# Recommendation tower on one core: the last group of gathers split in two, and a layer-2 step moved between two quarters of products

## What is computed

```
combined = concat([dense[:, None, :], e], axis=1)            # 512 x 27 x 128
inter    = einsum('bnd,bmd->bnm', combined, combined)        # 512 x 27 x 27
z = concat([dense, inter[:, triu_i, triu_j]], axis=1)
h = relu(concat([z, dense], axis=1) @ W_top1 + b_top1)       # 607 -> 512
h = relu(h @ W_top2 + b_top2)                                # 512 -> 256
y = h @ W_top3                                               # 256 -> 1
```

## Time and profile before

| | |
|---|---|
| median of 3 runs | 103.61 us (103.44 to 103.71) |
| the profiled execution | 104.75 us, of which its span 102.9 us and 1.85 us around it |
| TensorE busy, matmuls / weight loads | 95.2 us (92%) / 78.5 us (76%) |
| VectorE, ScalarE, GpSimd busy | 53.9 us (52%), 49.5 us (48%), 62.1 us (60%) |
| chain that ended last | PE 59%, DVE 19%, issue 6%, DMA 5%, POOL 5%, ACT 2% |
| mean granted TensorE clock | 0.983 |

### The profile page before, as it was taken

How to read it: one execution, slowest core, us unless ns; L and a number is a source line. 1 busy time by engine, 2 the same in 40 slices (tenths; PEclk the granted TensorE clock), 3 DMA queues, 4 the chain that set the end, 5 groups by cost and what they waited for, 6 DMA issues and landing times.

```text
span 102.9 us, 3492 instructions
## 1 busy us (share of the span) xinstructions
PE 95.2 (92%) x1525; PEld 78.5 (76%) x1525; DVE 53.9 (52%) x123; ACT 49.5 (48%) x85; POOL 62.1 (60%) x66
## 2 busy tenths in 40 slices
PE   5999999998999999999996999999899899399990
PEld 2348674886888888899886888998789798297870
DVE  4599999999999998953001600280026110043200
ACT  2845899969847966794110342052205621004250
POOL 1588877777777777777777777777777720000000
PEclk9999999999999999999999999999999999966999
DMA  2999999999999999942222222222222110000000
GB/s 70 261 253 262 248 291 234 245 253 232 252 248 220 236 245 356 367 117 49 57 59 53 57 56 53 57 54 57 57 51 57 51 51 0 6 6 0 6 0 1
DMA packets 5510, 13.46 MB, mean 131 GB/s; under 512 B 1748, under 2 KB 2264, under 8 KB 5367
## 3 DMA queue, kind: packets, MB, share of 16 engines
q1 hardware_dynamic: 3404, 9.11, 34.5%
q0 software_dynamic: 1920, 3.94, 14.8%
q10 hardware_dynamic: 170, 0.18, 0.8%
HBM read 13.23 MB, written 0.00 MB: 128 GB/s over the span
## 4 chain that ended last, share of the span: by engine, by line
PE 59%; DVE 19%; issue 6%; DMA 5%; POOL 5%; ACT 2%; POOLq 0%; DVEq 0%
PE ps_a L340 25%; DVE onehot L565 14%; PE ps_gram L377 10%; PE ps_a L425 6%; PE ps_rows L355 5%; DVE part_sb L574 5%; POOL rows_sb L313 5%; PE ps_h L439 5%; PE ps_a L402 3%; DMA idrow<-ids_by_table 3%; DMA rows_sb<-tbl,ids_sb 3%; PE ps_a L415 3%; PE ps_rows L452 2%; PE ps_h L465 1%; ACT table_sb L694 1%
## 5 line engine op out<-in xcount | busy, mean ns | idle before, releaser
L313 POOL DMA_INDIRECT rows_sb<-tbl,ids_sb x60 | 61.6, 1027 | 20.3 <-issue 16.5
L340 PE MATMUL ps_a<-onehot,part_sb 125*128 125x512 f32 (+1 forms) x208 | 45.2, 367 | 0.5 <-DVE part_sb L574 0.3
L340 PEld LDWEIGHTS ps_a<-onehot,part_sb 125*128 125x128 f32 x208 | 34.1, 188 | 8.5 <-DVE part_sb L574 2.2
L565 DVE TENSOR_SCALAR onehot<-idrow,row_id 125x1024 fp32r<-125x1024 int16 (+1 forms) x49 | 28.9, 644 | 1.9 <-DMA idrow<-ids_by_table 1.5
L377 PE MATMUL ps_gram<-xt 128*27 128x27 f32 x1024 | 13.3, 196 | 3.0 <-issue 2.8
L664 ACT COPY xt<-ps_rows 128x512 f32<-128x512 f32 (+1 forms) x16 | 9.8, 614 | 12.0 <-PE ps_rows L355 11.7
L377 PEld LDWEIGHTS ps_gram<-xt 128*27 128x27 f32 x1024 | 11.1, 108 | 5.6 <-issue 3.5
L574 DVE TENSOR_TENSOR part_sb<-table_sb,part_sb 125x512 fp32r<-125x512 f32 x22 | 14.4, 678 | 1.2 <-ACT part_sb L636 1.2
L657 ACT COPY xt<-ps_a 128x512 f32<-128x512 f32 (+1 forms) x13 | 7.5, 577 | 14.7 <-PE ps_a L340 14.7
L592 DVE STREAM_TRANSPOSE table_sb<-ps_gram 128x864 f32<-128x864 f32 x4 | 4.3, 1083 | 19.5 <-PE ps_gram L377 19.5
L636 ACT CAST part_sb<-table_sb 125x1024 fp32r<-125x1024 f32 (+1 forms) x13 | 11.7, 917 | 3.3 <-DMA table_sb<-tbl 3.3
(11 more groups left out here) (35 smaller groups left out, 41.4 us busy)
## 6 DMA issues: line engine op xcount, KB each, us to landing
table_sb<-tbl SPq DMA_DIRECT2D x11, 448.0 KB
w_sb<-w SPq DMA_DIRECT2D x1, 1280.0 KB, 10.9
idrow<-ids_by_table SPq DMA_DIRECT2D x4, 256.0 KB, 9.4
rows_sb<-tbl,ids_sb POOLq DMA_INDIRECT x60, 6.8
table_sb<-tbl SPq DMA_DIRECT2D x10, 52.0 KB
w_sb<-w SPq DMA_DIRECT2D x1, 512.0 KB, 11.5
idrow<-ids_by_table SPq DMA_DIRECT2D x2, 128.0 KB, 4.7
dense_sb<-dense_by_column SPq DMA_DIRECT2D x1, 256.0 KB, 7.9
```

What stands on the lines that cost most here:

```text
L313: pool.indirect_dma_start(rows_sb[:, t % ROWS_RING, k, :], None, tables[f], bass.IndirectOffsetOnAxis(ids_sb[:, t, f:f + 1], 0),).then_inc ...
L340: last = pe.matmul(ps_a[:, i % 2, a:b], parts_sb[part][:, w, c * D:(c + 1) * D], unit_onehot(u, c)[:, member, a:b], start=(part == HIGH an ...
L565: dve.tensor_scalar(unit_onehot(u, c), idrow[0:VP, w, 0:n, :], row_id[0:VP, first + c:first + c + 1], None, ALU.is_equal).then_inc(onehot_ ...
```

## The change

Group 15 is cut in two: group 15 now holds two tables and a new group 16 one. TensorE turns both in a row, ScalarE copies both in a row. In TensorE's list `layer2(2, 0)` moves from ahead of `turn_group(15)` to behind `gram(3, 0)`, and `layer2(2, 1)` moves from behind `gram(3, 3)` to the same place. The `min` in POOL's wait keeps the value for group 16 at what group 15 waits for (8).

```
@@ GROUPS
+_t, _first, _n = GROUPS.pop()
+GROUPS += [(_t, _first, _n - 1), (_t, _first + _n - 1, 1)]
@@ gpsimd
-                    pool.wait_ge(group_turned, g - ROWS_RING * len(GROUP_SIZES) + 1)
+                    pool.wait_ge(group_turned, min(g - ROWS_RING * len(GROUP_SIZES) + 1, (t - ROWS_RING + 1) * len(GROUP_SIZES)))
@@ tensor
             for m in range(M1):
                 layer1_pairs(2, m)
-            layer2(2, 0)
             turn_group(15)
+            turn_group(16)
             layer1_dense(3, 0)
             gram(3, 0)
+            layer2(2, 0)
+            layer2(2, 1)
             gram(3, 1)
             layer1_dense(3, 1)
             gram(3, 2)
             gram(3, 3)
-            layer2(2, 1)
@@ scalar
             copy_group(15)
+            copy_group(16)
             relu2(2)
```

## The result

| | changed | before | ratio (95% interval) |
|---|---|---|---|
| first measurement | 106.08 us (105.49 to 106.78, 4 runs) | 103.66 us (103.44 to 104.16, 4 runs) | 1.0219 (1.0168 to 1.027) |
| second, with later experiments | 103.91 us (103.05 to 106.34, 13 runs) | 104.25 us (103.1 to 105.4, 35 runs) | 0.998 (0.9936 to 1.0025) |

The changed kernel was slower by 2.2% in the first measurement, and could not be told from the one before in the second. The ratios leave out runs over 1.5% above the fastest of the same kernel, in the second measurement all four of the changed kernel at a low clock among them; medians, ranges and counts are over all runs.

The account below looks back on a forecast made before the run. TensorE was taken to hold the path, its largest pause 1.61 us of waiting for instructions. Terms of -0.55, -0.45 and -0.1 made -1.1 us, or -0.5 at full clock; the middle, -0.8, gave 102.8 us, range 102.3 to 104.6.

Parts of the forecast that it names:

- Products start 0.85 us earlier: Fourth tile: with `layer2(2, 0)` moved away and group 15 split, products start at 85.4, 0.85 us earlier (0.6 to 0.9).
- Layer 2 among the products, +2.0: Both halves of layer 2 between the first and second quarter of the fourth tile's products add 2.0 us.
- The pause, -1.6: TensorE's 1.61 us wait for instructions inside `gram(3, 2)` is filled by layer 2: -1.6 us, bounds 0 and -1.61.
- 3.6 us for a block, whatever stands in it: TensorE's next block of some 253 instructions is to be had 3.6 us after the current one begins, whatever its work.
- VectorE starts at 90.85: Fourth tile's products end and VectorE starts at 90.85 instead of 91.42, 0.55 us earlier.
- From there 2.4 us to layer 1: From VectorE's start to the last tile's layer 1: 2.4 us instead of 2.84, a gain of 0.45.
- The clock: Without the pause TensorE's clock stays full behind the last products; the products' end is some 0.1 us shorter.
- rival A: TensorE stands still behind the last products, half clock falls on the last tile: 104.5 us (103.9 to 104.8), chance 0.31.
- the middle, -0.8: Whole-kernel gain taken between -1.1 us (profiled execution, clock fallen) and -0.5 (clock full), giving 102.8 us.
- Rival B: Unprofiled runs wait less for instructions, so the pause among the products gives less: 103.5 us (103.2 to 103.9), chance 0.22.

Follow-up runs that it names:

- second half last: Changed kernel with `layer2(2, 1)` moved back behind the last products: 102.72 us, ratio 0.9829 against the kernel before; again 103.2 us, 0.9921.
- the gap filled: Changed kernel plus matmuls of zeros behind the last products: six gave 104.43 us, ratio 0.9989 against the kernel before; two gave 103.59 us, 0.9963.
- blocks shifted: Kernel before with its 13 warm-up matmuls of 512 columns cut into 52 of 128: 106.09 us, ratio 1.0081 against the kernel before.
- the split alone: Changed kernel with both halves of layer 2 back at their old places, groups 15 and 16 kept: 104.34 us, ratio 1.0045 against the kernel before.
- the move without the split: Kernel before with only `layer2(2, 0)` moved behind `gram(3, 0)`, group 15 whole: 103.46 us, ratio 0.9962 against the kernel before.

## Why the prediction was wrong

It forecast 102.8 us and a range to 104.6; 106.08 was measured. By its own steps:

1. *Products start 0.85 us earlier.* The mechanism was right, the size 0.7. In the changed kernel they start 1.24 us behind the first transpose's place (84.55 to 85.79), before it was 1.96 (84.29 to 86.25). I had 1.1; the last gather was issued at 82.46 instead of 82.07 and landed at 84.98, so the third transpose waited 0.18 us. Without that wait it is 1.03 (second half last: 84.61 to 85.64). That the split is what hides the landing stays untested.
2. *Layer 2 among the products, +2.0.* Right: 1.98 us.
3. *The pause, -1.6.* It went, as forecast, and the count of instructions was right. From the products' start to VectorE's the forecast had 5.45 us, and 5.33 was measured. So the term held in the sum; what is refuted is the rule behind it, "3.6 us for a block, whatever stands in it". The boundary lies some 31 matmuls into the fourth tile's products; in the kernel before the fetch moved data 1.1 us behind it, in the changed kernel 0.5 us behind it (boundary about 86.1, DMA at 86.6). With the second half last, the next boundary was reached at about 88.9 (88.72 + 18 x 0.01), 3.0 us behind the first, with hardly a pause. By my rule 0.7 us of the pause would have been left. So one half of layer 2 fills the block, and the second half was added to the path in full, 0.8 us by the comparison above. The sum had counted it in full too; the wrong rule hid that the better kernel was the one that moves one half.
4. *VectorE starts at 90.85.* Measured 91.12, with everything 0.26 us later from the start of the stretch. Right, against the profiled execution.
5. *From there 2.4 us to layer 1.* Right: 2.36. So steps 1 to 5 together held, the 0.13 us that step 1 missed being made up by step 3: the stretch is 8.93 us, where they give 8.96 (84.29 to 93.25).
6. *The clock. This is the step that failed.* I had it stay full behind the products, and held that likelier (0.47 to 0.31). In the four runs of the first measurement it fell in all: TensorE stood still for 1.58 us, half clock came at 93.5, and layer 1 took 4.47 us instead of 2.84. The price in the trace, 1.6 us, is the 1.7 of rival A. Between the two kinds of runs of the changed kernel it is 2.1 (105.5 against 103.35). Over both measurements the fall came in 8 of 17 runs, so neither case is the likeliest by much even now; with two such cases the range had to hold the dearer one whole.
7. *What the sum was set against, and the range.* The second error is "the middle, -0.8", between -1.1 for a profiled execution at low clock and -0.5 at full clock. The kernel before is at full clock in 63 of 64 runs, so -0.5 was the term to take; the traces at full clock show -0.2 to -0.45. Rival A's 104.5 was built on the -0.8. With 0.3 in its place and 1.6 to 2.1 for the clock it is 104.9 to 105.4, by an estimate from these numbers, and 106.08 is still 0.7 to 1.2 above that. Of the rest only this is known: I took the 0.27 us between three runs for the kernel's spread, and in 64 runs it is 102.99 to 106.04. And I read 1.14 us "missing" between the profiled execution and the median as a cost of being profiled. It is nothing of the kind: time less span is 1.8 to 1.9 us in every run (105.49 and 103.7; 104.46 and 102.7). The profiled execution was one of the few of the kernel before with a low clock, a poor one to take the sum from. Rival B rested on that reading, and it gave no ground for it; that the moved steps would simply cost what they take came half true, by step 3.

The Trainium skill's rule (TensorE: Matmul & The Clock Gate) that the chip judges the clock at moments of its own agrees with the runs: one kernel, four runs of 13 with the fall and nine without. In its two traces with the fall, half clock began 0.8 us behind the end of the still (92.66, 93.5) and 1.8 us behind it (93.56, 95.4). And the thirteen warm-up matmuls, begun at the same time, took 1.4 us less with the gap filled than with the second half last. That is what a rise of the clock at another moment would do, though the granted clock reads 1.00 there in both profiles:

```profile
1.19 4.34 PE L475 MATMUL ps_z<-zeros 128*128 128x512 bf16 x13 [1.19 <-DVE zeros L554]
...
1.19 5.73 PE L475 MATMUL ps_z<-zeros 128*128 128x512 bf16 x13 [1.19 <-DVE zeros L552]
```

What stays open: why the first four runs of the changed kernel all had the fall and were as slow as they were, what share a further set would have, and whether the chip matters, for the sets ran on different ones. Where the spread ahead of the stretch comes from, up to 2.4 us between runs of the kernel before at full clock, was not tried.

## What to carry to other kernels

Count instructions beside microseconds: where small matmuls use up a block faster than the next one can come, the engine stands still with no wait in sight. Independent work set into that block was free here up to about the length of the pause, and cost its full time beyond it. Work that keeps TensorE moving while another engine is waited for can be worth its place, even if nobody waits for it; moving it away may cost more than it takes. And before a forecast of under 1%, look at the granted clock of the one execution from which the sum is taken, and don't take the distance between three runs for the spread.

## What the runs showed of the hardware

- The next block of instructions was there 3.0 to 3.6 us after the one before it had begun. Pauses of 1.61, 1.47, 1.42 and 0.48 us at the last boundary among the products, and next to none (0.2 us or less), were seen in kernels that differ by where other work stands.
- One stretch at half clock costs 1.6 us on the path in the trace, 2.1 between the runs of the changed kernel, and 2.9 between those of the kernel with its blocks shifted. It came in 8 of 17 runs after a still of 1.58 us with three lone transposes behind it, and in 7 of 12 of the kernel with its blocks shifted, whose trace has a pause of 1.42 us and, 1.5 us of work later, a still of 0.5. Of the kernel before it came in 1 of 64 runs and in the execution that was profiled; there 1.2 us of products and 0.9 of layer 2 stand between the pause and the next still. It came in none of 24 with the gap filled by two or by six matmuls of zeros, and in none of the 42 of the split alone, the second half last and the move without the split.
